# A block of experts on one Trainium2 core, closed without GpSimd's drain

## What is computed

```python
x = x + _layernorm(_L0_attn_ref(_layernorm(x), Wc_down, Wq_up, Wkv_up, Wc_proj))
x = x + _layernorm(_L0_ffn_ref(_layernorm(x), centroids, ln_g, ln_b, W1, b1, W2, b2))
```

## Time and profile before

| | us |
|---|---|
| median of 3 runs | 868.62 |
| lowest, highest | 868.59, 870.29 |
| profiled execution, time | 868.64 |
| profiled execution, span | 866.9 |
| TensorE busy | 812.4 |
| VectorE busy | 641.0 |
| ScalarE busy | 548.7 |
| GpSimd busy | 294.8 |

### The profile page before, as it was taken

The page is one execution under the profiler, slowest core; times in us unless marked ns, Lnnn a source line. Parts: engine busy times, 40 slices in busy tenths (PEclk is TensorE's granted clock), DMA queues, the critical chain, the costliest instruction groups (busy, mean ns, idle before and its releaser), DMA issues. The chain is left out here.

```text
span 866.9 us, 20372 instructions
## 1 busy us (share of the span) xinstructions
PE 812.4 (94%) x5472; PEld 487.5 (56%) x5473; DVE 641.0 (74%) x2159; ACT 548.7 (63%) x1236; POOL 294.8 (34%) x547
## 2 busy tenths in 40 slices
PE   7989999999999999999999999379999999999993
PEld 3433333333333333333333348279999999999993
DVE  7899888988898989898988628745555555555552
ACT  4636667867677777677776766146666666666661
POOL 5412333244233432441233322033444444444211
PEclk9989999999999999999999999579999999999997
DMA  6204222321211111111153118930000100110000
GB/s 209 71 11 112 77 81 97 100 86 64 97 55 57 48 36 58 62 42 43 64 172 113 52 57 268 330 96 31 30 31 31 36 30 27 36 32 19 19 19 2
DMA packets 55764, 62.92 MB, mean 73 GB/s; under 512 B 13166, under 2 KB 47366, under 8 KB 55568
## 3 DMA queue, kind: packets, MB, share of 16 engines
q1 hardware_dynamic: 51952, 53.71, 19.2%
q0 software_dynamic: 3744, 8.40, 3.1%
HBM read 36.12 MB, written 9.57 MB: 53 GB/s over the span
## 5 line engine op out<-in xcount | busy, mean ns | idle before, releaser
L1192 ACT ACTIVATE W2s<-bank 128x512 f32<-128x512 f32 (+1 forms) x512 | 257.1, 572 | 117.2 <-PE bank L1084 115.0
L1252 DVE CUSTOM_DVE_ANT_0 room_kv<-bank,causal 128x384 bf16<-128x384 f32 (+3 forms) x512 | 220.7, 486 | 31.9 <-PE bank L1053 30.5
L1084 PE MATMUL bank<-W2s,room_kv 99*128 99x512 bf16 (+3 forms) x768 | 224.2, 330 | 4.5 <-ACT W1s L1192 3.0
L1053 PE MATMUL bank<-room_kv,W2s 96*128 96x512 bf16 (+3 forms) x768 | 218.5, 330 | 4.3 <-DVE R L1223 2.7
L1255 DVE TENSOR_REDUCE MP<-bank 128x1 f32<-128x512 f32 x256 | 162.8, 681 | 12.5 <-PE bank L1053 12.4
L1400 POOL TENSOR_SCALAR_AFFINE_SELECT W2s<-W2s 128x512 f32<-128x512 f32 x96 | 60.9, 635 | 286.5 <-ACT W2s L1192 284.3
L1084 PEld LDWEIGHTS bank<-W2s,room_kv 99*128 99x128 bf16 x768 | 67.9, 97 | 146.0 <-ACT W2s L1192 62.3
L1667 PEld LDWEIGHTS hp<-XNT,LT 128*128 128x128 f32 x1248 | 147.3, 194 | 3.3 <-DVE XNT L1744 1.4
L1667 PE MATMUL hp<-XNT,LT 128*128 128x128 f32 x1248 | 147.8, 277 | 1.0 <-DVE XNT L1744 1.0
L1675 PE MATMUL yp<-W2s,LT 128*128 x624 | 141.2, 379 | 0.6 <-DVE z L1755 0.6
L1101 PE MATMUL bank<-W2s,room_kv 128*32 128x512 f32 (+2 forms) x1152 | 129.4, 534 | 0.1
(11 more groups left out here) (189 smaller groups left out, 760.2 us busy)
## 6 DMA issues: line engine op xcount, KB each, us to landing
W2s<-W2s SPq DMA_DIRECT2D x160, 64.0 KB, 2.6
W1s<-in_L_ffn_W_dram SPq DMA_DIRECT2D x8, 1024.0 KB, 5.5
W2s<-in_L_ffn_W_dram SPq DMA_DIRECT2D x8, 1024.0 KB, 7.3
Y<-in_L_attn_x_dram SPq DMA_DIRECT2D x8, 512.0 KB, 7.7
Y<-W1s SPq DMA_DIRECT2D x32, 128.0 KB
W1s<-den_rows SPq DMA_DIRECT2D x16, 256.0 KB
LT<-in_L_attn_x_dram SPq DMA_DIRECT2D x8, 512.0 KB, 7.7
x_rows<-LT SPq DMA_DIRECT2D x8, 512.0 KB, 5.2
```

The source lines that it names most:

```text
L1053: last = pe.matmul(bank[:, at:at + w], Q[0:NR, g, i // BW, h, i % BW * P:(i % BW + 1) * P], K[b % 2][0:NR, k * NQ:k * NQ + w], start=True, ...
L1084: last = pe.matmul(dst[:, i, :], K[b % 2][0:KR, j * P:(j + 1) * P], Q[0:KR, g, c, h, off:NQ], start=True, stop=True)
L1192: act.activation(PR[t % RB][:, heads[0]:heads[-1] + 1, off:NQ], unit_of(ST[(NU * n + u) % STB], s), ACT.Exp, scale=SCALE).then_inc(exp_don ...
L1252: op = dve.tensor_tensor_reduce(junk[:, done % 2, at:at + w], src, causal[:, NQ - w:NQ], 1.0, LOWEST, ALU.add, ALU.max, dst)
```

## The change

The experts' block is opened with `no_gpsimd_drain=True`. With that option the engines other than GpSimd still drain at the block's end, GpSimd does not, and all five meet at a barrier made of semaphores alone. GpSimd's wait for all scatters stays in its place. Nothing else is touched, and the attention block is opened as before.

```diff
         scattered = sem("scattered")
         AHEAD = 3
 
-        block = ctx.enter_context(nc.Block())
+        block = ctx.enter_context(nc.Block(no_gpsimd_drain=True))
 
         def expert(eng, t):
```

## The result

The changed kernel takes 861.06 us (median of 4 runs, 860.5 to 861.15) against 868.61 us (4 runs, 868.11 to 870.29) for the kernel before: a ratio of 0.9905 with a 95% interval of 0.9891 to 0.9919. That is 7.55 us less, where about 6.45 us (the drain's length) had been forecast, and it lies 0.6 us under the low end of the range.

A forecast was written before the change was run, and what follows sets the result against it. Over the last 6.5 us GpSimd's closing drain alone was taken to set the end. 868.64 − 6.447 = 862.19, forecast 862.2 us; own range 861.8 to 862.8, whole range 861.7 to 868.9 us.

The forecast's parts named there:

- point 1: Experts' block end, line 1522: removing GpSimd's DRAIN, wholly on the path, takes 6.447 us off.
- point 3: Closing barrier at the block's end: changing to a semaphore-only one costs 0, bounds −0.25 to +0.25 us.
- points 2 and 4: Block's end: the wait for all scatters stays, end not before about 860.0; rest of the block: nothing changes.
- point 4: Experts' block ahead of its end: code and GpSimd's idle time stay the same, so no change in time.
- Rival A: Drain only moves, behind the span or to the next execution's first DRAIN; time stays about 868.6 us; chance 0.22.
- Rivals B and C: After the end, B: part owed, 864.2 us, chance 0.04; at program start, C: debt dearer, 870.5 us, chance 0.04.
- gap of 3.7 us: Between span and time: rival B's sign, against about 1.74 us if the forecast is right.
- first drain over 8.4 us: GpSimd's first DRAIN at program start: rival C's sign, against about 0.2 us if the forecast is right.
- C's factor: 1.325, first indirect DMA 1288 ns against last scatters 972; makes the drain at program start 8.54 us.

## Why the prediction was right and wrong

**The removed drain (point 1)** was right: it lay on the path whole. Its 6.447 us came off the end, and 6.445 came back when it was put back.

**The barrier (point 3)**, taken at 0 between bounds of −0.25 and +0.25 us, was right: 6.48 − 6.447 leaves 0.03 us. That the kernel with both the new barrier and a drain is at 1.0001 of the kernel before agrees, but its interval of some 1 us either way is wider than these bounds.

**What does not change (points 2 and 4)** was right for the instructions, and wrong for the time. The wait for the last landing stayed, and the drain's removal moved no work. But the sum takes the last scatter to start in the same place, at 858.00, and it started 1.11 us earlier, nearly all of it won around the stretch with another clock.

**The step that failed is the term of point 4: that ahead of the block's end nothing changes, put at nothing, and with nothing downward in the range of 861.8 to 862.8** (and so in the low end of 861.7 of the whole). Measured was 1.11 us in the first comparison, and the same changed kernel starts its last scatter anywhere from 856.49 to 859.61 in four profiled executions. I built the range from the barrier's bounds and put the runs' scatter on the upper side only, because three runs of the kernel before stood at 868.59, 868.62 and 870.29, and my sum went by a single profiled execution. That execution had a clock of 0.972, one of the lower draws. The kernel before takes from 866.55 to 871.85 us over the 80 later executions, and 25 of them have a clock of 0.977 or more and a median of 867.25. The scatter should have reached about 1.5 us downward as well (868.65, the median of 16 executions at 0.972, to 867.2 at 0.978), to 860.7, and 861.06 lies within that. The clock's view by itself gave a hint, since a mean under 1 says that stretches at half clock exist, and their place might shift.

The size of the drain's part was right: 868.22, the median of the 80 executions, less 6.447 is 861.77 us, and the 19 of the changed kernel have 861.64. That the first four lay lower still, all at 0.981 or 0.982, was no part of the mechanism. Whether it was chance, or the change makes these patterns likelier, stays open.

**Rival A**, the drain only moves, is out for this kernel's measured time. The first DRAIN of the program in the changed kernel:

```profile
L1826 POOLq EVENT_SEMAPHORE  x2: 17/17/17, 0.6 to 0.7; - x2
...
L1826 POOLq DRAIN  x1: 188/188/188, 0.4 to 0.4; - x1
```

188 ns, as in the earlier trace rows, and 186 to 189 in the other kernels without a drain at their end. Nor did it move behind the span: the time stands above the span by a median of 1.78 us in the 19 executions of the changed kernel and 1.76 us in the 80 of the kernel before. With that the reset of the DMA rings behind a kernel, which the Trainium skill lists on its page "Runtime: NRT & Kernel Launch", section "The ~15µs preamble/postamble breakdown", takes nothing of the gain back: whatever that reset does, no row or run here shows it waiting for GpSimd. Rival A rested on the guess that the drain settles something owed. That it does some work for each DMA is true; that anybody in this program or in the time behind it has to pay for it is not. Whether it is done ahead of the first instruction of a next execution, outside what is measured, stays open.

**Rivals B and C** both need A's debt and went with it: no gap of 3.7 us between span and time, and no first drain over 8.4 us. C's factor was also drawn too high: it sets the first gather against scatters, and against the other gathers of the earlier trace rows it is 1288 / 998 = 1.29, which gives a drain of 8.3 us.

By the Trainium skill's page "VectorE: DVE Perf Modes", section "The DRAIN you can't avoid", the DRAINs that the runtime puts around a kernel take a constant 12 ns or so. The closing one is not of that kind. Its length is no constant: 34, 706 and 6447 ns, by what GpSimd had issued.

## What to carry to other kernels

Look at what only the sequencers execute behind the last instruction of the timeline: the chain of waits ended 7.9 us before the span did, and most of the difference, 6.4 us, was one GpSimd drain at a price of 82 ns for each DMA that GpSimd had issued. If every DMA has been waited for, leave the drain out. If it has to stay, drain once more where GpSimd has time; the last one then has only the DMAs since then to pay for. Letting the drain run beside the last landing, by leaving out the wait, saved 1.2 us here, but that a drain makes sure of a landing was not shown, so the wait is the safe choice. And before a range is drawn round a small effect, take the scatter of the unchanged kernel from many executions with their clocks, on both sides.

## What the runs showed of the hardware

A GpSimd drain in this kernel costs about 50 ns and 82 ns for each indirect DMA issued since the last drain (716, 706 and 6447 ns after 8, 8 and 78, and 5.15 us after 62), although these had been waited for (all but the last of the 62), and whether a DMA moved 64 or 128 rows (701 against 716 ns). A drain right behind another takes 34 ns. It does its work beside a transfer that is still under way (7.51 us from 857.92, of which 6.45 lie behind the end of the last scatter's execution, with the landing at about 860.0). The same program is granted a mean clock between 0.971 and 0.978 from one execution to the next, and takes 866.55 to 871.85 us (medians 868.65 us at 0.972, 869.01 at 0.974 and 867.2 at 0.978); its stretches at the lower clock lie in different places from one execution to the next. What decides between the patterns is not shown.
